# Context attention with its scores computed twice: once plain for the maxima, once with keys on partitions and the maximum taken off inside the product

## The chip, the cores and the metric

One core of a Trainium2 chip runs the whole program in one launch. The metric is the device time of one execution in microseconds (us), lower is better. PE is TensorE, DVE is VectorE, ACT is ScalarE, POOL is GpSimd, SP is the queue that issues most transfers.

## The reference, cut to what matters

The program is a chain of eight residual layers over x of shape (8, 256, 256). The change touches the third alone, an attention in which each of 256 tokens of a batch looks at 256 context tokens and the batch's own 256 tokens. There is no mask in this layer.

```python
def _L1_xattn_ref(x, context, w_qkv, w_proj, b_proj):    # x is layer-normed, (8, 256, 256)
    ...
    q, k, v = (qkv[0], qkv[1], qkv[2])                    # 16 heads of 16
    ...
    k = jnp.concatenate([extra_k, k], axis=2)             # 512 keys
    v = jnp.concatenate([extra_v, v], axis=2)
    attn = jnp.einsum('bhnd,bhmd->bhnm', q * scale, k)
    attn = jax.nn.softmax(attn, axis=-1)
    out = jnp.einsum('bhnm,bhmd->bhnd', attn, v)
    return out @ w_proj.T + b_proj
```

## The kernel before, in words

Activations lie with features on partitions. `context_attention_layer` first runs a layer norm, then one block in which all engines stream through the eight batches. The block is written by `attention_stream`; names of its tiles begin with `ca_`.

The work is cut into iterations: 8 per batch (R), 64 in all (NR). An iteration takes 128 queries (half of a batch's) and four heads, which lie on the four 32-row strips of the partitions: strip u holds heads 2u and 2u+1 of its half, 16 rows each, and the iteration takes the even or the odd one of each strip. The four score products of 128 queries by 512 keys go to four PSUM banks, one per head.

- **PE** makes the four scores (`scores`, line 753), each on its own strip of 32 rows. In batch 0 the operands are plain (`ca_k`, `ca_qz`, where the other head's 16 rows of queries are zero). From batch 1 on they are `HalfStack`'s: queries and keys are split into a rounded part and a rest, both parts of a head stand in one strip, and two products per head in the faster float32r type make one score. Then PE turns the exponentials, 16 transposes of 128x128 per iteration (`turn`, line 767), and every second iteration multiplies them with the values (`values`, line 791), 16 products, each on its own 32 columns of the array.
- **DVE** takes the negated maximum of each score row (line 963) and copies two of the four turned banks of an iteration to SBUF (line 969). **ACT** makes the exponential with the maximum as its bias and the row sum as a second output (line 896) and copies the other two turned banks (line 905).
- The reciprocal of the sums is widened on POOL (line 722), turned by PE (line 810), copied by ACT and multiplied into the output by DVE (line 997). `project` (line 1298) and the addition to the stream (line 1311) follow.
- `HalfStack` costs POOL two casts and three subtractions a batch (lines 1382 to 1394) and SP 24 small transfers a batch that move 16-row halves within SBUF (lines 1403 and 1411).
- The next batch's queries, keys and values (`front`, PE lines 1324 and 1340) are made in iterations 0, 4 and 6 of a batch.

Each engine's order is written out by hand. An engine executes in order, and a wait stops all that stands behind it. A transposing or score product that refills a bank waits for whoever read it last:

```python
for u in range(u0, u0 + GA):
    if n > 0:
        pe.wait_ge(exped, 4 * (n - 1) + u + 1)     # scores: bank u is free when its exponential is done
...
pe.wait_ge(exped, 4 * n + last + 1)                # turn: needs the exponential
pe.wait_ge(copied_v if f % 2 == 0 else copied_a, (fill - 2) // 2 + 1)
```

## Time and profile before

| | |
|---|---|
| median of 3 runs | 2622.49 us (2622.3 to 2631.82) |
| the profiled execution's own time | 2618.37 us |
| its span, first to last instruction | 2616.5 us |
| TensorE's mean granted clock | 0.964 of full |
| the block with the change, first score to last addition | 463.44 to 799.40, 335.96 us |

### The profile page before, as it was taken

What the parts mean: (1) busy time and instruction counts of PE and PEld (TensorE: products, weight loads), DVE (VectorE), ACT (ScalarE), POOL (GpSimd) and SP (SyncE); (2) the same over time, 40 slices, a digit from 0 to 9 for tenths busy, and PEclk for the clock granted to TensorE, in tenths of its full rate; (3) what the DMA queues carried; (4) which work ended last, traced back from release to release, by engine and by line L of the source; (5) the groups of instructions that cost most, each with busy time, mean ns of one, the idle gap of its engine ahead of it and who ended that gap; (6) DMA issues with size and microseconds to landing.
All of it is one profiled execution on the core that took longest, in us unless ns stands there. A gap on an engine that the chain in (4) does not pass through costs nothing. (4 is left out here: it accounts for less than half of the span.)

```text
span 2616.5 us, 38185 instructions
## 1 busy us (share of the span) xinstructions
PE 2261.1 (86%) x14797; PEld 1623.2 (62%) x14797; DVE 1313.9 (50%) x2690; ACT 985.1 (38%) x2815; POOL 175.7 (7%) x227
## 2 busy tenths in 40 slices
PE   6778887899988999989999999997998888773884
PEld 4455565566655666666666666665886666552773
DVE  6456565688885344433554454456443554543003
ACT  3245564677773111121333233344221444323222
POOL 0000000122200000000000000003001000002003
PEclk8979999999999999999999999998999999997997
DMA  3000000122112000021000000001002000004332
GB/s 118 17 1 1 1 1 22 42 53 50 38 29 97 0 1 1 1 83 40 9 9 9 9 9 1 1 1 29 1 1 71 25 17 19 1 1 142 127 131 69
DMA packets 62833, 83.43 MB, mean 32 GB/s; under 512 B 10936, under 2 KB 49088, under 8 KB 61760
## 3 DMA queue, kind: packets, MB, share of 16 engines
q1 hardware_dynamic: 61120, 76.80, 9.5%
q0 software_dynamic: 1536, 4.20, 0.6%
q8 instruction: 121, 1.98, 0.3%
q14 instruction: 56, 0.46, 0.1%
HBM read 65.24 MB, written 8.39 MB: 28 GB/s over the span
## 5 line engine op out<-in xcount | busy, mean ns | idle before, releaser
L896 ACT ACTIVATE ca_prob<-bank,ca_nmax 128x512 f32<-128x512 f32 x256 | 174.0, 690 | 75.0 <-DVE ca_nmax L963 75.0
L896 ACT ACTIVATE na_prob<-bank,na_nmax 128x257 f32<-128x257 f32 x256 | 118.0, 474 | 192.3 <-DVE na_nmax L963 192.3
L963 DVE TENSOR_REDUCE ca_nmax<-bank 128x1 f32<-128x512 f32 x256 | 164.2, 683 | 42.0 <-PE bank L753 42.0
L1596 PE MATMUL bank<-rf_W,rf_h 128*128 128x256 f32 x768 | 170.8, 379 | 0.0
L1585 PE MATMUL bank<-XN,rf_W 128*128 128x512 f32 x384 | 170.1, 593 | 0.0
L1596 PEld LDWEIGHTS bank<-rf_W,rf_h 128*128 128x128 f32 x768 | 146.0, 190 | 33.0 <-issue 14.8
L896 ACT ACTIVATE ra_prob<-bank,ra_nmax 128x256 f32<-128x256 f32 x256 | 118.2, 482 | 105.3 <-DVE ra_nmax L963 105.3
L1640 ACT ACTIVATE rf_r<-bank 128x512 f32<-128x512 f32 x96 | 57.3, 597 | 261.1 <-PE bank L1585 261.1
L767 PE MATMUL bank<-cst,ca_prob 128*128 128x128 f32 x1024 | 141.5, 280 | 7.6 <-DVE ca_pT L969 5.9
L767 PEld LDWEIGHTS bank<-cst,ca_prob 128*128 128x128 f32 x1024 | 111.8, 142 | 54.1 <-issue 45.4
L963 DVE TENSOR_REDUCE na_nmax<-bank 128x1 f32<-128x257 f32 x256 | 90.9, 417 | 91.5 <-PE bank L753 91.5
L1786 PE MATMUL bank<-na_cxT,na_Wkv 128*128 128x256 f32 x512 | 117.8, 383 | 5.6 <-DVE na_q L1780 5.6
L1585 PEld LDWEIGHTS bank<-XN,rf_W 128*128 128x128 f32 x384 | 72.4, 190 | 78.6 <-issue 77.3
L1904 PE MATMUL bank<-sf_h,sf_W 128*128 128x512 f32 x512 | 120.1, 395 | 0.0
L1692 DVE TENSOR_TENSOR rf_h<-rf_r 128x512 f32<-128x512 f32 x96 | 66.1, 692 | 104.4 <-ACT rf_r L1640 104.4
L1798 PE MATMUL bank<-na_Wkv,na_cxT 128*128 128x512 f32 x256 | 115.4, 595 | 0.0
L1786 PEld LDWEIGHTS bank<-na_cxT,na_Wkv 128*128 128x128 f32 x512 | 95.1, 190 | 25.9 <-DVE na_q L1780 11.9
L1904 PEld LDWEIGHTS bank<-sf_h,sf_W 128*128 128x128 f32 x512 | 96.0, 188 | 23.5
L233 PE MATMUL bank<-ln_rstd,cst 128*128 128x128 f32 x352 | 51.9, 291 | 51.7 <-DVE ln_rstd L319 51.7
L969 DVE COPY ca_pT<-bank 128x512 f32<-128x512 f32 x128 | 87.6, 684 | 17.1 <-PE bank L767 16.7
L1705 DVE SCALAR_TENSOR_TENSOR rf_acc<-bank,rf_comb,rf_acc 128x256 f32<-128x256 f32 x112 | 49.0, 479 | 90.9 <-PE bank L1596 90.9
L963 DVE TENSOR_REDUCE ra_nmax<-bank 128x2 f32<-128x512 f32 x128 | 82.1, 683 | 22.1 <-PE bank L753 22.1
(404 smaller groups left out, 4349.3 us busy)
## 6 DMA issues: line engine op xcount, KB each, us to landing
xl_w<-in_L_ffn_w SPq DMA_DIRECT2D x16, 1024.0 KB, 7.5
dp_cx<-in_ctx_tok SPq DMA_DIRECT2D x4, 1024.0 KB, 14.7
ca_v<-in_ctx_values SPq DMA_DIRECT2D x8, 512.0 KB, 4.7
rf_W<-in_L_ffn_w SPq DMA_DIRECT2D x8, 512.0 KB, 9.1
na_Wkv<-in_L_xattn_Wkv SPq DMA_DIRECT2D x1, 4096.0 KB, 16.0
na_cxT<-in_ctx SPq DMA_DIRECT2D x8, 512.0 KB, 3.4
ma_cxT<-in_ctx SPq DMA_DIRECT2D x8, 512.0 KB, 3.3
ca_q_halves<-ca_q_halves SPq DMA_DIRECT2D x112, 32.0 KB, 2.0
```

Source lines behind the costliest of these rows:

```text
L233: mm = pe.matmul(bank[:, c * P:(c + 1) * P], pick[:, c * P:(c + 1) * P], of, start=True, stop=True)
L767: mm = pe.transpose(TB[f % 2][:, j * P:(j + 1) * P], prob[:, n % 2, u, c0:c0 + P], ident)
L896: e = act.activation(prob[:, n % 2, u, hh * keys:(hh + 1) * keys], S[u][:, hh * keys:(hh + 1) * keys], ACT.Exp, bias=nmax[:, n % 2, u, hh: ...
L963: v.tensor_reduce(nmax[:, n % 2, u], S[u][:, 0:W].rearrange("p (h k) -> p h k", h=per), AX.X, ALU.max, negate=True).then_inc(maxed, 1)
L969: v.tensor_copy(o, TB[f % 2][:].rearrange("p (j q) -> p j q", j=4)).then_inc(copied_v, 1)
L1585: mm = pe.matmul(g.bank[n % 3][:], W1[:, k, c * P:(c + 1) * P], g.XN[:, k, gi * GT:(gi + 1) * GT], start=(k == 0), stop=(k == KD - 1))
L1596: mm = pe.matmul(output(i, t), h[:, n % 8, t * P:(t + 1) * P], W2[:, n % CH], start=(n == own[0]), stop=(n == own[-1]), skip_group_check=True)
L1640: act.activation(r[:, n % 3], g.bank[n % 3][:], ACT.Relu).then_inc(relu, 1)
L1692: v.tensor_tensor(h[:, n % 8], r[:, n % 3], r[:, n % 3], ALU.mult).then_inc(squared, 1)
L1786: mm = pe.matmul(bank[:, m * N:(m + 1) * N], Wkv[:, k, (m0 + m) * P:(m0 + m + 1) * P], cxT[:, b % 2, k], start=(k == 0), stop=(k == KC - 1))
L1798: mm = pe.matmul(bank[:], cxT[:, b % 2, k, t * P:(t + 1) * P], Wkv[:, k, INNER + half * 512:INNER + (half + 1) * 512], start=(k == 0), sto ...
L1904: mm = pe.matmul(g.bank[m % 4][:], W1[:, k, m * P:(m + 1) * P], h[:, k, s], start=(k == 0 and s == 0), stop=(k == C1 - 1 and s == 1))
```

## The change: what it does

`attention_stream` loses its `stack` argument, `HalfStack` goes, and the layer calls a new function, `key_major_stream`, with the same 64 iterations plus ten to drain it.

- The scores are made once as in the old batch 0 (plain operands, 128 queries by 512 keys, float32), for the maxima alone. They use a ring of three banks (0 to 2), which they share with one transpose per iteration.
- DVE writes the negated maxima of the four heads into four columns of an otherwise zero tile `ca_Z` (128x128). PE turns it once (`turn_maxima`), and DVE adds it to the queries: `ca_qa` (`shift_queries`). The maximum of a head then stands in a row of the other head's half of the strip. POOL forms a second copy of the keys, `ca_kf`, in which that row is 1.
- Three iterations later PE makes the scores again with keys on partitions: 128 keys by all 256 queries, the maximum already taken off (`turned_score`). Two tiles of keys per head and iteration fill a bank of a ring of three (3 to 5). ACT makes the plain exponential of a bank, 128x512, straight into `ca_pT`. Nothing is turned or copied behind it, and no sum is taken by ACT.
- The values' empty columns hold 0.25, so that the product with the values (8 per iteration) yields the sums as rows of the output bank. Per half batch ACT copies that bank, two transfers take the sums to 64 partitions each, DVE makes the reciprocals, a third transfer takes them to 8 rows, PE spreads them in one product, and DVE multiplies. POOL masks and adds the two halves of the output.

On PE each iteration has two mixed groups: two scores on two strips, and two heads of turned scores, two tiles of keys each, on the other two. In code (waits for a batch's start left out):

```diff
+            def score(n, u):
+                ...
+                if at[e] >= 3:
+                    pe.wait_ge(taken, at[e] - 2)
+                pe.matmul(score_bank(e)[:], qz[32 * u:32 * u + 32, b % 2, odd, m, i * P:(i + 1) * P],
+                          kk[32 * u:32 * u + 32, b % 2, m, :], start=True, stop=True).then_inc(scored, 1)
+            def turned_score(t, j, c):
+                ...
+                if c == 0:
+                    if pos >= 3:
+                        pe.wait_ge(exped, pos - 2)
+                    pe.wait_ge(taken, at[("z", 2 * (t // 2) + 1)] + 1)
+                tile = 2 * (t % 2) + c
+                mm = pe.matmul(g.bank[3 + pos % 3][:, c * N:(c + 1) * N],
+                               kf[32 * u:32 * u + 32, b % 2, m, odd, tile * P:(tile + 1) * P],
+                               qa[32 * u:32 * u + 32, odd], start=True, stop=True, skip_group_check=True)
+            def pair(n, first_unit):
+                t = n - 3
+                ...
+                if n < NR:
+                    score(n, first_unit)
+                    score(n, first_unit + 1)
+                if 0 <= t < NR:
+                    for c in range(2):
+                        turned_score(t, j0, c)
+                        turned_score(t, j0 + 1, c)
+            def turn_maxima(n):
+                e = ("z", n)
+                pe.wait_ge(taken, max(at[e] - 2, at[("s", n, 3)] + 1))
+                pe.transpose(score_bank(e)[:, 0:P], Z[:, (n // 2) % 2, n % 2], ident).then_inc(scored, 1)
+            for n in range(ITER):                       # PE
+                pair(n, 0)
+                if 1 <= n <= NR:
+                    turn_maxima(n - 1)
+                for use in slots[n][0]:                 # spread, project
+                    shared(use)
+                pair(n, 2)
+                if 0 <= n - 4 < NR:
+                    values(n - 4)
+                for use in slots[n][1]:                 # front
+                    shared(use)
+            for n in range(ITER):                       # DVE
+                if n < NR:
+                    maximum(n, 0)
+                    maximum(n, 1)
+                if 1 <= n <= NR:
+                    shift_queries(n - 1)
+                for use in slots[n][0]:
+                    shared(use)
+                if n < NR:
+                    maximum(n, 2)
+                    maximum(n, 3)
+                ...                                     # reciprocal of a half batch
+                for use in slots[n][1]:
+                    shared(use)
-        stack = HalfStack(g, sb, kk)
-        attention_stream(g, ctx, "ca", 16, 16, groups, 2 * N, front, (0, 4, 6), q_of, k_of,
-                         ...
-                         stack=stack)
+        key_major_stream(g, ctx, wl, 3, load, front, (0, 4, 6), qz, kk, vv, project(Wp, KD), add_to_stream(g, bias))
```

`at[e]` is a score's or a turned maximum's place in the order s0, s1, z, s2, s3 of an iteration, and its bank is `at[e] % 3`.

How PE's order changes, in the middle of a batch: before, two iterations of the stream (a score product per head and part, then transposes).

```order
L753 MATMUL bank<-ca_k_halves,ca_q_halves 128x512 x8
L767 MATMUL bank<-cst,ca_prob 128x128 x16
L753 MATMUL bank<-ca_k_halves,ca_q_halves 128x512 x8
L767 MATMUL bank<-cst,ca_prob 128x128 x8
L791 MATMUL bank<-ca_pT,ca_v 32x256 x16
L767 MATMUL bank<-cst,ca_prob 128x128 x8
```

Of the change, one iteration at the same place: L1497 is a plain score, L1509 a turned one, L1537 the turned maxima, L1563 the spread of the reciprocals, L1548 the values.

```order
L1497 MATMUL bank<-ca_k,ca_qz 128x512 x2
L1509 MATMUL bank<-ca_qa,ca_kf 128x256 x4
L1537 MATMUL bank<-cst,ca_Z 128x128
L1563 MATMUL bank<-ca_inv_rows,cst 128x256
L1497 MATMUL bank<-ca_k,ca_qz 128x512 x2
L1509 MATMUL bank<-ca_qa,ca_kf 128x256 x4
L1548 MATMUL bank<-ca_pT,ca_v 32x256 x8
```

The 16 transposes of an iteration are one, the eight float32r products are four plain ones, and eight turned scores have come. They stand behind the second pair of plain scores.

DVE's order before, some two iterations with the multiplication of a batch's output (L997):

```order
L963 TENSOR_REDUCE ca_nmax<-bank 128x1 x2
L969 COPY ca_pT<-bank 128x4x128
L997 TENSOR_TENSOR ca_outT<-bank,ca_spread 128x512
L963 TENSOR_REDUCE ca_nmax<-bank 128x1 x2
L969 COPY ca_pT<-bank 128x4x128
L963 TENSOR_REDUCE ca_nmax<-bank 128x1 x2
L1311 SCALAR_TENSOR_TENSOR X<-bank,ca_bias,X 128x256 x2
```

And of the change, from the addition to the queries (L1642) to the first maxima of the iteration after the one in which the next batch's queries are taken (L1307):

```order
L1642 TENSOR_TENSOR ca_qa<-ca_qz,bank 128x128
L1659 TENSOR_TENSOR ca_outT<-bank,ca_data 128x256
L1632 TENSOR_REDUCE ca_Z<-bank 128x1 x2
L1307 TENSOR_SCALAR ca_qz<-bank,cst 128x512 x2
L1632 TENSOR_REDUCE ca_Z<-bank 128x1 x2
```

The copies of turned banks are gone, a small addition per iteration has come, and the queries of the next batch, two operations in place of one, stand ahead of the maxima.

## Rows read from the trace of the kernel before

**Rows 1.** The cores.

```profile
core 0: 2616.5 us, clock 0.964
```

**Rows 2.** Stretches: from:to, length, each engine's busy us (instructions), clock, DMA.

```profile
463.44:503.90 40.46, 33.76 (x268) 21.19 (x272) 27.68 (x46) 26.85 (x72) 7.95 (x6) 0.96 0.15 27
503.90:543.90 40.00, 36.95 (x364) 26.78 (x356) 32.55 (x56) 31.13 (x81) 8.56 (x7) 1.00 0.21 47
763.90:799.40 35.50, 27.11 (x280) 18.25 (x280) 22.30 (x37) 21.21 (x54) 0.61 (x1) 1.00 0.00 1
463.44:799.40 335.96, 299.62 (x2856) 211.72 (x2856) 261.40 (x437) 250.94 (x655) 60.45 (x50) 0.99 0.17 37
```

**Rows 3.** Groups of instructions between 460 and 800 us.

```profile
L896 ACT ACTIVATE ca_prob<-bank,ca_nmax 128x512 f32<-128x512 f32 x256 | 174.0, 690 | 75.0 <-DVE ca_nmax L963 75.0
L963 DVE TENSOR_REDUCE ca_nmax<-bank 128x1 f32<-128x512 f32 x256 | 164.2, 683 | 42.0 <-PE bank L753 42.0
L767 PE MATMUL bank<-cst,ca_prob 128*128 128x128 f32 x1024 | 141.5, 280 | 7.6 <-DVE ca_pT L969 5.9
...
L969 DVE COPY ca_pT<-bank 128x512 f32<-128x512 f32 x128 | 87.6, 684 | 17.1 <-PE bank L767 16.7
L905 ACT ACTIVATE ca_pT<-bank 128x512 f32<-128x512 f32 x128 | 77.0, 601 | 2.8 <-PE bank L767 2.8
...
L753 PE MATMUL bank<-ca_k_halves,ca_q_halves 32*128 32x512 f32 x448 | 41.4, 439 | 21.0 <-ACT ca_prob L896 21.0
...
L1298 PE MATMUL bank<-ca_outT,ca_Wp 128*128 128x256 f32 x64 | 15.7, 389 | 1.6 <-DVE ca_outT L997 1.6
L1340 PE MATMUL bank<-ca_Wqkv,XN 128*128 128x256 f32 x64 | 15.1, 379 | 0.0
```

**Rows 4.** Timeline of an iteration in batch 2: start, length, engine, work.

```profile
582.13 0.74 PE L753 MATMUL bank<-ca_k_halves,ca_q_halves 32*128 32x512 f32 x8 [0.52 <-ACT ca_prob L896]
...
583.82 1.93 PE L791 MATMUL bank<-ca_pT,ca_v 128*32 128x256 f32 x32
...
587.01 0.74 PE L753 MATMUL bank<-ca_k_halves,ca_q_halves 32*128 32x512 f32 x8 [0.23 <-ACT ca_prob L896]
```

**Rows 5.** Timeline of an iteration in batch 0, plain scores.

```profile
473.52 1.14 PE L753 MATMUL bank<-ca_k,ca_qz 32*128 32x512 f32 x8 [0.71 <-ACT ca_prob L896]
...
474.60 1.09 PE L767 MATMUL bank<-cst,ca_prob 128*128 128x128 f32 x8
474.65 1.29 DVE L963 TENSOR_REDUCE ca_nmax<-bank 128x1 f32<-128x512 f32 x2 [1.59 <-PE bank L753]
...
475.86 0.68 DVE L969 COPY ca_pT<-bank 128x512 f32<-128x512 f32 x1
...
476.69 1.40 PE L767 MATMUL bank<-cst,ca_prob 128*128 128x128 f32 x8 [1.00 <-DVE ca_pT L969]
```

**Rows 6.** Stretches of batch 0 around a change of clock, columns as in Rows 2.

```profile
475.79:479.20 3.41, 1.66 (x12) 1.18 (x16) 2.54 (x5) 3.35 (x10) 0.00 (x0) 1.00 0.25 54
479.20:482.60 3.40, 3.40 (x20) 1.77 (x16) 2.14 (x4) 1.42 (x5) 0.00 (x0) 0.50 0.18 38
```

**Rows 7.** Timeline, the taking of batch 0's queries and the block's last work.

```profile
459.25 1.41 DVE L1460 TENSOR_SCALAR ca_qz<-bank,cst 128x512 f32<-128x512 f32 x2 [4.15 <-PE bank L1324]
...
791.92 1.93 PE L791 MATMUL bank<-ca_pT,ca_v 128*32 128x256 f32 x32 [0.78 <-ACT ca_pT L905]
...
798.52 0.88 DVE L1311 SCALAR_TENSOR_TENSOR X<-bank,ca_bias,X 128x256 f32<-128x256 f32 x2 [2.15 <-PE bank L1298]
```

**Rows 8.** A small DVE addition's nearest neighbour, another layer's.

```profile
L1008 DVE TENSOR_TENSOR ra_rq<-ra_rq,cst 128x80 f32<-128x80 f32 x16 | 3.2, 239 | 0.3
```

**Rows 9.** DMA issues: tiles, queue, count, KB each, median us to landing.

```profile
ca_k_halves<-ca_k_rest SPq DMA_DIRECT2D x56, 64.0 KB, 2.3
```

More of the change, by code:

```diff
@@ L53, in shape_constants @@
     parts["even16"] = np.concatenate([0.25 * ((p // 16) % 2 == 0), 0.25 * ((p // 16) % 2 == 1)], axis=1)
+    parts["keep_one"] = np.concatenate([p % 32 != 16, p % 32 == 16, p % 32 != 0, p % 32 == 0], axis=1)
+    parts["head_row"] = (f // 16 == 2 * (p % 4) + p // 4)
     parts["half5"] = np.where(p < REG, 0.5, 1.0)
@@ L558, in attention_stream @@
                      wl, n_weights, mask=None, own_keys=False, load=None, n_loads=0, load_after=None, null=None, reg=None,
-                     stack=None,
                      divide=False):
@@ L684, in _ @@
                     if b >= 2:
-                        if stack is not None:
-                            stack.move_queries(sp, b)
                         load_after(sp, b - 2, ready, ready_at, valued, R)
@@ L689, in _ @@
                         d.then_inc(ld[b % 2], 16)
-                    if stack is not None and b >= 1:
-                        if b == 1:
-                            stack.move_queries(sp, b)
-                        stack.move_keys(sp, b)
             sp.wait_ge(wl, 16 * n_weights)
@@ L697, in _ @@
         def _(po):
-            def split_keys_and_queries(b):
-                wait_freed(po, ("front", b, 0))
-                if b >= 2:
-                    po.wait_ge(scored, 4 * R * (b - 1))
-                stack.split_queries(po, b)
-                po.wait_ge(ld[b % 2], 16 * n_loads * (b // 2 + 1))
-                stack.split_keys(po, b, slice(0, N))
-                wait_freed(po, ("front", b, 1))
-                stack.split_keys(po, b, slice(N, 2 * N))
             for n in range(NR):
                 f, r2 = divmod(n, RF)
-                if stack is not None and n % R == 0 and n // R + 1 < B:
-                    split_keys_and_queries(n // R + 1)
                 if null is not None:
@@ L735, in scores @@
                         pe.wait_ge(ld[b % 2], 16 * n_loads * (b // 2 + 1))
-                    if stack is not None and b >= 1:
-                        stack.wait_stacked(pe, b)
                 for u0 in range(0, 4, GA):
@@ L745, in scores @@
                             pe.matmul(S[u][:, 0:W], ml, mr, start=True, stop=False, skip_group_check=True)
-                    parts = 2 if stack is not None and b >= 1 else 1
                     for hh in range(per):
-                        for part in range(parts):
-                            for u in range(u0, u0 + GA):
-                                i, a, hs = unit(n, u)
-                                q = q_of(hs[hh], i, b) if parts == 1 else q_of(hs[hh], i, b, part)
-                                last = hh == per - 1 and part == parts - 1
-                                mm = pe.matmul(S[u][:, hh * keys:(hh + 1) * keys], q, k_of(hs[hh], i, b),
-                                               start=(mask is None and part == 0), stop=last, skip_group_check=True)
-                                if last:
-                                    mm.then_inc(scored, 1)
+                        for u in range(u0, u0 + GA):
+                            i, a, hs = unit(n, u)
+                            mm = pe.matmul(S[u][:, hh * keys:(hh + 1) * keys], q_of(hs[hh], i, b), k_of(hs[hh], i, b),
+                                           start=(mask is None), stop=(hh == per - 1), skip_group_check=True)
+                            if hh == per - 1:
+                                mm.then_inc(scored, 1)
             def turn(n, f):
@@ L1425, in context_attention_layer @@
         bias = sb("bias", [P, KD])
-        qz = sb("qz", [P, 2, KD, N])
+        qz = sb("qz", [P, 2, 2, KD, N])
         kk = sb("k", [P, 2, KD, 2 * N])
@@ L1438, in prepare @@
             for j in range(2):
-                po.memset(vv[:, j, 2:4], 0.0).then_inc(zeroed, 1)
+                po.memset(vv[:, j, 2:4], 0.25).then_inc(zeroed, 1)
             po.wait_ge(zeroed, 2)
@@ L1447, in load @@
                                A["ctx_values"][b * N:(b + 1) * N, :].rearrange("(t p) d -> p t d", p=P))
[L1449 to L1489 removed]
+        front = qkv_front(g, Wqkv, qz, g.c("even16"), lambda b: kk[:, b % 2, :, N:2 * N], lambda b: vv[:, b % 2, 2:4])
+        key_major_stream(g, ctx, wl, 3, load, front, (0, 4, 6), qz, kk, vv, project(Wp, KD), add_to_stream(g, bias))
 def routed_ffn_layer(g):
@@ L2542 @@
     lay["L2_null_values"] = nv.reshape(P, 128)
-    cv = _np.zeros((T, 8, 4, 16), _np.float32)
+    cv = _np.full((T, 8, 4, 16), 0.25, _np.float32)
     cv[:, :, 0] = c[:, D:].reshape(T, 8, 2, 16)[:, :, 0]
```

331 lines of the change are left out of this document (258 added, 73 removed).

## Prediction

> **What bounds the kernel now.** I read the cores first: one core, 2616.5 us, clock 0.964 [rows 1]; the execution's own time is 2618.4 us, 4.1 below the median of the three runs. Then the stretches of the block [rows 2]. It lasts 335.96 us, and a batch in the middle takes 40.0 us, in which PE is busy 36.95, DVE 32.55, ACT 31.13 and POOL 8.56. PE is the bound, though not by much. The groups of instructions [rows 3] say what PE does: transposes of the exponentials 141.5 us of 299.6, scores 41.4, the front, the values and the projection. The timeline [rows 4] shows an iteration from score to score: 587.01 - 582.13 = 4.88 us. PE's waits there are short (0.52, 0.23), because while one iteration's maxima and exponentials are made, PE turns those of the iteration before: 2.2 us of work of its own that does not depend on them. That cover is what the reader is to keep in mind.
>
> **What goes.** Per iteration 16 transposes (141.5/64 = 2.2 us of PE), two copies by DVE (87.6/64 = 1.37) and two by ACT (77.0/64 = 1.20) [rows 3], eight float32r products (0.74 us, [rows 4]), POOL's splits and SP's 24 transfers a batch. POOL and SP were off the path.
>
> **What comes on PE.** A plain score group stands in batch 0 [rows 5]: four heads on four strips, two passes each, start at 473.52, and the next work of PE starts at 474.60: 1.08 us. A mixed group of the change fills the same four strips with as many columns (512 on two of them, 2 x 256 on the other two), so it should take 1.08 as well, if the two kinds overlap as four alike do. In the mixed group two more waits stand between the strips' products, and no row prices them; between nothing and 0.2 us I take 0.12, so 1.20. Two groups are 2.3 to 2.4 us. The turned maxima are one transpose, 1.09/8 = 0.14 [rows 5]. The values are half of 1.93 per iteration [rows 4], 0.97, the same per head as before. PE's own work is then 2.2 + 0.14 + 0.97 = 3.3 us against 0.74 + 2.2 + 0.97 = 3.9 before. By work alone the change saves 0.6 us an iteration.
>
> **What comes as a wait.** The second group's second score, s3, refills the bank of s1, three places earlier in the ring, and so waits until DVE has taken the maximum of s1. The turned scores of the second group stand behind s3 in PE's queue, the values behind those, the front behind the values. So PE's chain of an iteration, without front, is:
> - first group's start to DVE's first maximum: 474.65 - 473.52 = 1.13 [rows 5];
> - two maxima: 1.29 [rows 5];
> - DVE's end to PE's start: 475.86 + 0.68 = 476.54, to 476.69 = 0.15 [rows 5];
> - s3 and the turned scores behind it: 1.20 (1.08 at the least);
> - the values: 0.97; then the next first group finds its banks free (the maximum of s2 ended about 0.9 us before).
>
> Together S = 4.74 us (4.62 to 4.9). PE stands still for some 1.3 us in the middle, with only s2 under way in part of it. The transposes that covered this wait before are what the change removes; the turned scores could cover it, but stand behind it.
>
> **Off the path.** DVE's addition to the queries is 128x128; its nearest row is 128x80 in 0.24 us [rows 8], and DVE is idle there. ACT's exponential loses its sum and bias, between 0.60 (a copy of the same bank) and 0.69 [rows 3]; four are 2.4 to 2.8 us of 4.74. The ring of exponential banks waits for exponentials made 1 us or more before, in the worst case by 0.1. The transfers of the sums: 2.3 us to landing for 64 KB moved within SBUF [rows 9]; two hops, a copy and a reciprocal are about 7 us and have five iterations. If that cover went, DVE's next maxima would wait behind the reciprocal; I see no shortage. The spread, 0.5 us, fits in PE's gap.
>
> **The sum over the block.**
> - 60 iterations (4 to 63) at 4.74: 284.4.
> - Front: 21 products of 15.1/8 = 1.89 [rows 3] stand behind the values, on the path; one lies under DVE's work at the start: 37.8.
> - Taking the queries: two DVE operations in 1.41 [rows 7] where the next maximum is due after 1.13, so 0.4 late, six times: 2.4.
> - Projection 15.7/8 = 1.96 [rows 3] in a gap of about 1.35: 0.6, six times: 3.6.
> - Iterations 0 to 2, DVE's four maxima and an addition: 3 x 3.2 = 9.6; iteration 3, S without values: 3.8.
> - Iterations 64 to 66, turned scores, exponentials, values: 3 x 3.8 = 11.4.
> - The end: last exponentials and values, copy, two hops at some 2.4, reciprocal, spread, multiplication, projection, addition: 11.5. Before, the last values to the end took 799.40 - 791.92 = 7.5 [rows 7].
>
> Sum 364.5 against 335.96: +28.5. On the execution's own 2618.4 that is 2647; beside the median, 2651.
>
> **Rivals.**
> *PE stays the bound* (0.10, faster). If the wait for DVE is covered, a batch costs PE 8 x 3.3 + 5.7 (front) + 2.0 + 1.0 = 35.1 us of work in place of 36.95; with the old idle time of 3 us, 38.1 against 40.0. Over 7.5 batches that is -14, and POOL and SP give nothing: 2608. For it speaks that DVE and ACT each lose over 1 us an iteration, against it the ring of three banks. It decides at S: 60 S + 80 = 336 gives S = 4.26, so the gap would have to be 0.5 us shorter than I make it.
> *About no change* (0.12). The gap closes part of the way, by s2 and the spread lying in it and groups nearer 1.0; S of 4.2 to 4.4 gives 2619 to 2631, 2622 where it breaks even.
> *The clock falls* (0.15, slower still). In batch 0 PE was busy 1.66 of 3.41 us, and in the next 3.40 us the granted clock was 0.50, the lower of the two levels, 1.2 GHz [rows 6]; the middle batches, with PE busy 92%, kept 1.00 [rows 2]. The change brings an idle gap in each iteration. Each such 3.40 us gives up 1.7; once a batch is +14, 2665, once in three iterations +34, 2685.
> *The passes don't overlap in mixed groups* (0.08, far slower). If every product waited for both passes of the one ahead of it in program order, s0 and s1 would need 1.5 us and the turned scores another 0.75, 2.25 a group. The second group would still start at 1.13 + 1.29 + 0.15 = 2.57, and the chain is then 2.57 + 2.25 + 0.97 = 5.8, +1.05 x 60: 2714. Four heads alike show the opposite: eight passes of about 0.5 us each in 1.08 [rows 5].
> The Trainium skill, "TensorE: Matmul & The Clock Gate", step-by-step list of Part 2, says that only weight loads are pulled ahead and that the "MATMULs themselves stay in program order". By that rule the group in batch 0 would take about 2.5 us; the trace disagrees with 1.08, and the sum stays with the trace.
>
> **How the numbers follow.** My forecast has 0.55, and its own range is 2638 to 2668: S from 4.62 to 4.9 is -7 to +10, the ends and the front a few us. The rivals have 0.10, 0.12, 0.15 and 0.08. The range of 8 in 10 leaves out the faster case and the passes that don't overlap, which is 0.18, and reaches through the clock's case and most of no change: 2624 to 2690. What a measurement of this kernel can tell from no change is 0.5%, 13 us: faster below 2609, slower above 2636. Faster: 0.10. Same: 0.12 and the lower edge of my own, 0.17. Slower: 0.73.
>
> **What the profile of the changed kernel would show.** PE idle before L1497, ended by DVE's maxima (L1632), once an iteration and about 0.6 to 1.3 us long: over 50 us in all. From a first group to the next without front, 4.7 us. A mixed group of 1.1 to 1.2 us from its first start to PE's next work. DVE and ACT each below 30 us of a batch's 44. No waits for the transfers of sums except at the end. Clock near 1.00 in the middle batches. It is wrong if the idle time before L1497 is small, if a group takes over 1.5 us, or if the clock falls in the middle batches.

## The result, and the profile after

The changed kernel takes 2675.6 us (median of 4 runs, 2673.61 to 2677.25). The kernel before, timed with it, takes 2627.15 us (2622.3 to 2633.11, 4 runs). The ratio is 1.0183, 95% interval 1.0154 to 1.0212, so the change costs 48.5 us where 28.5 were forecast. That lies in the wide range of 2624 to 2690 us, but above my own forecast's, which ended at 2668. The direction was right. The steady part of the block was right too, and its start and end were not.

The first view is the cores of the changed kernel, beside [rows 1].

```profile
core 0: 2674.7 us, clock 0.955
```

The second is its windows, columns as in [rows 2]: the first 42 us of the block, two batches in the middle, and the block.

```profile
466.54:508.90 42.36, 39.68 (x197) 22.85 (x198) 20.81 (x36) 9.28 (x17) 2.49 (x4) 0.72 0.00 1
508.90:553.56 44.66, 40.90 (x360) 24.57 (x362) 25.03 (x48) 19.16 (x35) 8.09 (x10) 1.00 0.07 19
598.22:642.88 44.66, 42.01 (x368) 25.59 (x368) 26.12 (x51) 19.16 (x35) 8.10 (x10) 1.00 0.07 20
466.54:845.42 378.88, 349.25 (x2888) 210.05 (x2888) 207.62 (x396) 152.67 (x279) 61.23 (x76) 0.96 0.05 14
```

The block takes 378.88 us against 335.96, +42.9. A middle batch takes 44.66 against 40.0 at a full clock, with DVE and ACT busy 26 and 19 us of it, so no engine but PE could be the bound by its work alone. The first 42 us ran at a mean clock of 0.72.

The third view is the groups of instructions of the block.

```profile
L1497 PE MATMUL bank<-ca_k,ca_qz 32*128 32x512 f32 x512 | 183.5, 663 | 22.9 <-DVE ca_Z L1632 21.8 <-DVE ca_v L1326 1.1
L1632 DVE TENSOR_REDUCE ca_Z<-bank 128x1 f32<-128x512 f32 x256 | 165.1, 686 | 110.5 <-PE bank L1497 109.4
L1509 PE MATMUL bank<-ca_qa,ca_kf 32*128 32x256 f32 x1024 | 154.1, 405 | 0.7 <-ACT ca_pT L1592 0.7
L1592 ACT ACTIVATE ca_pT<-bank 128x512 f32<-128x512 f32 x256 | 138.9, 594 | 199.1 <-PE bank L1509 199.1
L1548 PE MATMUL bank<-ca_pT,ca_v 128*32 128x256 f32 x1024 | 69.2, 389 | 0.0
...
L1497 PEld LDWEIGHTS bank<-ca_k,ca_qz 32*128 32x128 f32 x512 | 56.9, 188 | 80.7 <-DVE ca_Z L1632 63.7 <-issue 15.5 <-DVE ca_v L1326 1.4
```

DVE waits for scores (109.4 us), and the weight loads of the scores wait for DVE (63.7 us): each waits for the other. PE itself shows only 21.8 us of idle time before L1497, because a score on another strip is still under way in part of the wait. The timeline of one iteration in batch 2 shows that.

```profile
602.75 0.70 PE L1497 MATMUL bank<-ca_k,ca_qz 32*128 32x512 f32 x2
...
602.77 0.70 PE L1509 MATMUL bank<-ca_qa,ca_kf 32*128 32x256 f32 x4
...
603.29 0.59 PE L1497 MATMUL bank<-ca_k,ca_qz 32*128 32x512 f32 x2
603.30 0.60 PE L1509 MATMUL bank<-ca_qa,ca_kf 32*128 32x256 f32 x4
...
603.83 0.33 PE L1537 MATMUL bank<-cst,ca_Z 128*128 128x128 f32 x1
603.91 1.29 DVE L1632 TENSOR_REDUCE ca_Z<-bank 128x1 f32<-128x512 f32 x2 [1.57 <-PE bank L1497]
...
604.65 0.29 PEld L1497 LDWEIGHTS bank<-ca_k,ca_qz 32*128 32x128 f32 x2 [0.28 <-DVE ca_Z L1632]
...
605.25 0.18 PEld L1497 LDWEIGHTS bank<-ca_k,ca_qz 32*128 32x128 f32 x1 [0.31 <-DVE ca_Z L1632]
...
605.36 0.79 PE L1509 MATMUL bank<-ca_qa,ca_kf 32*128 32x256 f32 x4
...
605.81 1.29 DVE L1632 TENSOR_REDUCE ca_Z<-bank 128x1 f32<-128x512 f32 x2
...
606.51 1.07 PE L1548 MATMUL bank<-ca_pT,ca_v 128*32 128x256 f32 x16
607.51 1.99 PE L1300 MATMUL bank<-XN,ca_Wqkv 128*128 128x256 f32 x8
609.44 0.70 PE L1497 MATMUL bank<-ca_k,ca_qz 32*128 32x512 f32 x2
```

Read from the top: the group starts, 1.16 us later DVE begins, 1.29 later both maxima are taken, s3's weights load at 605.25, the turned scores behind it and s3 end at 606.51, and the values take 1.00 to the front at 607.51. That is 4.76 us where 4.74 were forecast.

The fourth view is the windows around the changes of clock at the start and the end of the block.

```profile
462.82:469.66 6.84, 4.98 (x22) 2.76 (x21) 2.66 (x6) 0.60 (x1) 4.08 (x6) 1.00 0.02 7
469.66:473.07 3.41, 3.41 (x8) 2.32 (x8) 0.68 (x1) 0.00 (x0) 0.00 (x0) 0.50 0.00 0
473.07:476.48 3.41, 2.63 (x11) 1.22 (x11) 2.80 (x6) 0.00 (x0) 0.00 (x0) 1.00 0.00 0
476.48:496.96 20.48, 20.40 (x82) 11.77 (x79) 9.88 (x17) 4.34 (x8) 0.00 (x0) 0.50 0.00 1
...
831.48:838.31 6.83, 2.74 (x36) 1.16 (x34) 0.68 (x2) 1.56 (x3) 2.54 (x3) 1.00 0.03 5
838.31:845.13 6.82, 4.94 (x10) 3.02 (x10) 1.02 (x3) 0.00 (x0) 0.00 (x0) 0.50 0.00 0
```

The granted clock was 0.50, the 1.2 GHz level, for 23.9 us in the first iterations and for 6.8 us over the last spread and projection. Each time PE had been idle for part of the stretch ahead. Before, batch 0 had one such stretch of 3.40 us [rows 6].

**Where the 42.9 us are.** I marked each iteration by its turned maxima (L1537). From the sixth of them to the last, 58 iterations, the chip took 317.3 us and my sum has 316.8. The steady part was right. From the first score to the sixth turned maxima it took 37.1 us and my sum has 26.0: +11.1. From the last turned maxima to the last addition the sum was 2.8 short. With 0.5 in the middle that is the whole 14.4 between the forecast +28.5 and +42.9. Outside the block the start comes 3.1 us later than before. The layer norm behind it takes as long as before. The 16 products of the next layer's router (L1566, now L1796) take 1.5 us more, 3.32 us at a mean clock of 0.54 where they took 1.85 us at 1.00.

The two profiled executions differ by more, 58.9 us. Of that, 9.3 lie in the last expert layer, which took 225.1 us in the profile before and 234.4 in this one. The change doesn't touch it, and in profiles of other kernels below it took 227 to 238, so the profile before was a short one of its kind: 2618.37 us beside a median of 2627.15. The layer's length goes with its granted clock: 225.1 us at a mean of 0.86, 227.4 at 0.85 (e7), 234.4 at 0.82, 237.9 at 0.80 (e4). No edit was made there, so this is seen and not tested. I compare medians for the total and records for the block.

### The profile page after: what moved, and what is told of

Its sections match the earlier page's. It is cut to its first block and busy times, and to the rows that moved or that the text cites. A ratio compares the mean times of both kernels' runs of the same rounds, so it can differ in the third digit from the quotient of the medians.

```text
span 2674.7 us, 37814 instructions
## 1 busy us (share of the span) xinstructions
PE 2323.0 (87%) x14829; PEld 1630.3 (61%) x14829; DVE 1260.7 (47%) x2650; ACT 887.8 (33%) x2439; POOL 180.1 (7%) x257
## 5 line engine op out<-in xcount | busy, mean ns | idle before, releaser
L1632 DVE TENSOR_REDUCE ca_Z<-bank 128x1 f32<-128x512 f32 x256 | 165.1, 686 | 110.5 <-PE bank L1497 109.4
L1592 ACT ACTIVATE ca_pT<-bank 128x512 f32<-128x512 f32 x256 | 138.9, 594 | 199.1 <-PE bank L1509 199.1
L1497 PE MATMUL bank<-ca_k,ca_qz 32*128 32x512 f32 x512 | 183.5, 663 | 22.9 <-DVE ca_Z L1632 21.8
L1509 PE MATMUL bank<-ca_qa,ca_kf 32*128 32x256 f32 x1024 | 154.1, 405 | 0.7 <-ACT ca_pT L1592 0.7
L1497 PEld LDWEIGHTS bank<-ca_k,ca_qz 32*128 32x128 f32 x512 | 56.9, 188 | 80.7 <-DVE ca_Z L1632 63.7
L1509 PEld LDWEIGHTS bank<-ca_qa,ca_kf 32*128 32x128 f32 x1024 | 99.7, 188 | 6.2 <-ACT ca_pT L1592 2.3
```

What stands on the lines that cost most here:

```text
L1497: pe.matmul(score_bank(e)[:], qz[32 * u:32 * u + 32, b % 2, odd, m, i * P:(i + 1) * P], kk[32 * u:32 * u + 32, b % 2, m, :], start=True, s ...
L1509: mm = pe.matmul(g.bank[3 + pos % 3][:, c * N:(c + 1) * N], kf[32 * u:32 * u + 32, b % 2, m, odd, tile * P:(tile + 1) * P], qa[32 * u:32 * ...
L1592: act.activation(pT[:, t % 2, TURN[j]].rearrange("p c q -> p (c q)"), g.bank[3 + pos % 3][:], ACT.Exp)\
L1632: v.tensor_reduce(Z[:, odd, n % 2, col:col + 1], score_bank(e)[:], AX.X, ALU.max, negate=True)\
```

## The experiments

All start from the changed kernel. I give them by what they tell apart, not in the order in which they ran. In the table, "against before" is the difference to the median of the kernel before, timed with it on the same chip, "58 iterations" is from the sixth to the last turned maxima, "start" from the first score to the sixth, "block" from the first score to the last addition, in us.

| kernel | median | against before | ratio, 95% | start | 58 iterations | block |
|---|---|---|---|---|---|---|
| changed | 2675.60 | +48.5 | 1.0154 to 1.0212 | 37.1 | 317.3 | 378.9 |
| e1 | 2663.97 | +36.1 | 1.0086 to 1.0148 | 34.9 | 294.6 | 360.8 |
| e2 | 2670.45 | +42.6 | 1.0142 to 1.0177 | 37.0 | 306.6 | 368.0 |
| e3 | 2643.36 | +15.5 | 1.0032 to 1.0075 | 30.9 | 290.0 | 345.4 |
| e4 | 2671.98 | +44.1 | 1.0133 to 1.0179 | 28.6 | 317.3 | 369.9 |
| e5 | 2704.55 | +81.1 | 1.0277 to 1.0324 | 35.6 | 347.3 | 407.2 |
| e6 | 2676.30 | +52.8 | 1.0174 to 1.0217 | 37.2 | 317.7 | 379.5 |
| e7 | 2667.58 | +44.1 | 1.0152 to 1.0200 | 30.6 | 318.0 | 373.1 |
| e8 | 2666.85 | +43.4 | 1.0138 to 1.0183 | 28.6 | 317.3 | 368.3 |
| e9 | 2646.21 | +19.9 | 1.0042 to 1.0095 | 34.6 | 284.9 | 344.8 |
| e10 | 2659.16 | +32.8 | 1.0089 to 1.0138 | 35.4 | 301.3 | 362.9 |
| e11 | 2644.67 | +18.3 | 1.0046 to 1.0084 | 28.1 | 301.3 | 353.5 |
| e12 | 2679.28 | +53.0 | 1.0158 to 1.0215 | 35.6 | 320.3 | 380.4 |
| e13 | 2657.63 | +31.9 | 1.0064 to 1.0129 | 30.8 | 302.0 | 359.6 |
| e14 | 2647.05 | +21.3 | 1.0045 to 1.0092 | 27.6 | 290.6 | 344.4 |
| e15 | 2635.72 | +10.0 | 1.0014 to 1.0044 | 26.9 | 290.6 | 341.3 |
| e16 | 2663.52 | +37.8 | 1.0090 to 1.0156 | 27.7 | 312.1 | 367.6 |

Theory A is the prediction's: PE stands still in each iteration because a score must wait for the maximum of the score three places earlier in its ring of banks. The main rival is that PE's own work bounds the iteration. A second question is the clock at the ends.

**e3, half as much work for DVE.** A maximum looks at 256 of the 512 keys, so its result can be another one.

```diff
-                v.tensor_reduce(Z[:, odd, n % 2, col:col + 1], score_bank(e)[:], AX.X, ALU.max, negate=True)\
+                v.tensor_reduce(Z[:, odd, n % 2, col:col + 1], score_bank(e)[:, 0:N], AX.X, ALU.max, negate=True)\
```

> Each maximum is taken over the first 256 of the 512 scores of its row (this leaves out part of the maximum; the scores themselves are all made). A maximum should take about 0.41 us for 0.68, and two back to back about 0.76 for 1.29. Theory A: the two maxima lie on the chain once per iteration, so -0.5 us x 60 = -30, about 2645. Theory B (PE is the bound) or C (the clock): 2670 to 2680, as DVE is idle half the time.

The timeline of e3, two maxima and the turned maxima of two iterations:

```profile
599.69 0.33 PE L1537 MATMUL bank<-cst,ca_Z 128*128 128x128 f32 x1
599.77 0.76 DVE L1632 TENSOR_REDUCE ca_Z<-bank 128x1 f32<-128x256 f32 x2 [1.16 <-PE bank L1497]
...
603.91 0.33 PE L1537 MATMUL bank<-cst,ca_Z 128*128 128x128 f32 x1
```

Two maxima take 0.76 us in place of 1.29, and the iteration 4.22 in place of 4.76: 0.54 shorter, as much as the maxima, although DVE was busy for little more than half of the time. The maxima are on PE's path, and the whole came to -33 us: 27 of the 33.5 us by which the block shrank are in the 58 iterations, 6 at its start, where 13.7 us ran at a clock of 0.50 for 23.9 in the changed kernel.

**e12, work for PE where it stands still.**

```diff
+                if 3 < n < NR:
+                    free = 4 * (n - 3) + 2
+                    pe.wait_ge(exped, free - 2)
+                    pe.matmul(g.bank[3 + free % 3][:, 0:N], ident, g.XN[:, 0, 0:N], start=True, stop=True, skip_group_check=True)
                 pair(n, 2)
```

> The changed kernel with one unread 128x256 product (0.5 us of PE) in each of iterations 4 to 63, between the turned maxima and the second group. If PE stands idle there for DVE (theory A), the 60 products cost nothing: 2676, within 2 us of the changed kernel. If PE's work bounds the iteration (rival B), they cost up to 60 x 0.5 = 30 us: 2706.

An iteration stayed at 4.76 us. The 60 products cost 3.0 us over the 58 iterations, nearly all of it in the seven iterations with a projection, where PE's gap is filled already (6.01 us there, the changed kernel has 5.58). The rival's 30 us are not there. The total came out 4.5 us above the changed kernel's, more than the 2 expected.

**e1, the values moved into the gap.**

```diff
                 for use in slots[n][0]:
                     shared(use)
-                pair(n, 2)
                 if 0 <= n - 4 < NR:
                     values(n - 4)
+                pair(n, 2)
```

> The values product of an iteration is issued between the turned maxima and the second group instead of behind it; nothing else moves. Theory A (the chain: first group, two maxima, second group, values, each waiting for the one before): the values, 0.97 us, now lie in PE's idle gap of about 1.3 us, the iteration falls from 4.76 to about 3.9 us, over 60 iterations -52 us, so about 2623, no slower than the kernel before. Theory B (PE itself is the bound in the steady part, groups of mixed strips simply cost more than the transposes did): the order changes nothing, 2670 to 2680. Theory C (the whole excess is the clock at the start and end of the block): the same 2670 to 2680.

This missed: -12 us where theory A said -52. The timeline of e1 shows where the gap's place was taken.

```profile
603.74 0.70 PE L1497 MATMUL bank<-ca_k,ca_qz 32*128 32x512 f32 x2
...
604.90 2.60 DVE L1632 TENSOR_REDUCE ca_Z<-bank 128x1 f32<-128x512 f32 x4 [1.63 <-PE bank L1497]
...
605.64 0.18 PEld L1497 LDWEIGHTS bank<-ca_k,ca_qz 32*128 32x128 f32 x1 [0.74 <-DVE ca_Z L1632]
...
606.90 0.33 PE L1537 MATMUL bank<-cst,ca_Z 128*128 128x128 f32 x1
607.16 1.07 PE L1548 MATMUL bank<-ca_pT,ca_v 128*32 128x256 f32 x16
608.16 0.70 PE L1497 MATMUL bank<-ca_k,ca_qz 32*128 32x512 f32 x2
```

The group of 603.74 is now the second one. Behind it comes the next iteration's first group with nothing between, and its second score needs the bank of s2. So the wait stands at s1, for the first maximum of the pair. The iteration is 1.16 + 0.65 + 0.18 to s1, a group of 1.17, the turned maxima 0.26 and the values 1.00: 4.42 us. The projection lost its gap too: the iteration with it went from 5.58 to 6.58. My expectation had moved the work and forgotten the wait on the other side of the ring.

**e2, the second group turned round.**

```diff
-                if n < NR:
+                if n < NR and first_unit == 0:
                     score(n, first_unit)
                     score(n, first_unit + 1)
                 if 0 <= t < NR:
                     ...
+                if n < NR and first_unit == 2:
+                    score(n, first_unit)
+                    score(n, first_unit + 1)
```

> In the second group of an iteration the turned scores are issued ahead of the two plain scores; nothing else moves. The turned scores then fill the gap, but the two plain scores still wait for both maxima and the values still wait for them. Theory A: the chain keeps 1.13 + 1.29 + 0.15 + 1.08 + 0.97 = 4.6 of its 4.76 us, so -7 to -10 us, 2666 to 2669. A rival (what stands behind the waiting score is what costs, so PE gains all the work that is moved ahead of it, about 1 us an iteration): about 2615. Theory B or C: 2670 to 2680.

An iteration took 4.55 us in place of 4.76, and the 58 iterations 10.7 less. The median went down by 6, a little less than the 7 to 10 expected. The turned scores cover part of the wait, as expected.

**e5 and e6, the fourth score late.** e5 issues s3 behind the values and the front:

```diff
                 pair(n, 2)                                  # now without score(n, 3)
                 if 0 <= n - 4 < NR:
                     values(n - 4)
                 for use in slots[n][1]:
                     shared(use)
+                if n < NR:
+                    score(n, 3)
```

> From the changed kernel: the fourth score of an iteration, s3, is issued behind the values (and the front), directly ahead of the next iteration's first group, all else as in the changed kernel. Theory A (the ring of three score banks stops PE at s3, and e1 missed because with the values in the gap the same wait stood at the next s1, behind s2's maximum): s3 is now reached after about 1.15 + 0.26 + 0.7 + 1.0 = 3.1 us, when its bank has been free since 2.57, so PE's wait before s3 goes. What is left is the turned maxima, which need the maximum of s3: s3's group about 1.3, its maximum 1.13 + 0.65 + 0.15 behind s3's start, so 0.6 of idle time; iteration 1.95 + 0.26 + 0.7 + 1.0 = 3.9 us without front, about 6 us a batch less than 44.66 with front and projection on the path, 2625 to 2640 in all. Rival B (the iteration is bound by the work of PE and DVE together, and e3 was faster only because DVE had less work): the iteration stays above 4.3, and the time above 2650.

e6 also issues four of the eight products with the values between `pair(n, 0)` and `turn_maxima(n - 1)`.

> As e5, and the values of an iteration in two halves of four products: one between the first group and the turned maxima, one behind the second group. Theory A: the first half (0.5 us) covers most of the 0.6 us that PE would wait for the turned maxima in e5; iteration 3.4 to 3.7 us without front, a batch 36.5 to 38.5, total 2605 to 2625, so under the kernel before. Rival B: as for e5, no faster than 2650. Rival C: another ring stops it next (the exponentials' banks, or s1 behind the maximum of s2), iteration 3.8 to 4.0 as in e5, total 2625 to 2640.

Both missed, e5 by 65 us and e6 by 51. The timeline of e5, in an iteration behind one with a front:

```profile
608.96 0.69 DVE L1635 TENSOR_REDUCE ca_Z<-bank 128x1 f32<-128x512 f32 x1 [3.49 <-PE bank L1497]
...
610.23 1.28 DVE L1635 TENSOR_REDUCE ca_Z<-bank 128x1 f32<-128x512 f32 x2
610.96 0.18 PEld L1497 LDWEIGHTS bank<-ca_k,ca_qz 32*128 32x128 f32 x1 [1.11 <-DVE ca_Z L1635]
```

The one maximum at 608.96 is that of the late s3. It stands ahead of the next iteration's maxima in DVE's queue, so s2, which refills the bank of s0, waits for DVE to reach it: from the group's start 1.16, two maxima 1.29, 0.15, a group 1.2 and the values 1.0 are 4.8 us, the same chain as before with another score at its end (4.76 measured). With a front in the iteration the maxima come later again. Those longer waits had a second effect: the clock fell in the middle of the block. It was 0.50 for 30.7 us of e5's 58 iterations, for example for 13.7 us from 523.10 on, where PE had been idle for 1.6 of the 6.8 us before. So a part of e5's loss is the clock and not the chain. In e6 half of the values lies in the wait, 4.38, and it loses that in the iterations with front and projection.

**e9 and e10, the values split around the second group.**

```diff
                     turn_maxima(n - 1)
+                if 0 <= n - 4 < NR:
+                    values(n - 4, range(0, 4))              # e10: range(0, 6)
                 for use in slots[n][0]:
                     shared(use)
                 pair(n, 2)                                  # now s2, turned scores, s3
                 if 0 <= n - 4 < NR:
-                    values(n - 4)
+                    values(n - 4, range(4, 8))              # e10: range(6, 8)
```

> From the changed kernel: four of an iteration's eight products with the values are issued ahead of the second group, between the turned maxima and it; and in the second group the turned scores stand between s2 and s3. Theory A (PE's chain runs over two waits of one ring, s3 behind the maximum of s1 and the next s1 behind that of s2; e1, e5 and e6 each moved PE's work so that the other wait took over): the start of the first group to s3 is 1.13 + 1.29 + 0.15 = 2.57 as before, and behind it stand s3 alone, about 1.0, and half of the values, 0.5: 4.05 us without front against 4.76, about 40 us in the block, 2633 to 2640. Rival B (a mixed group can't be cut up without loss, or s3 alone takes as long as a group): 4.4 and more, 2655 or above.

> As e9 with six of the eight products ahead of the second group. Theory A: 2.57 + 1.0 + 0.25 = 3.85 us an iteration, 5 to 12 us below e9, 2625 to 2632; if the next s1 then waits for the maximum of s2, as in e1, 4.0 to 4.1 and the same time as e9.

e9's iterations came as worked out: 3.99 and 4.12 us, a batch 40.2, 34 us less in the block. The total is 29 us under the changed kernel's and 6 above the range expected. e10 was slower, and not 5 to 12 us faster. Its timeline:

```profile
604.77 0.63 PE L1551 MATMUL bank<-ca_pT,ca_v 128*32 128x256 f32 x4
604.85 1.29 DVE L1638 TENSOR_REDUCE ca_Z<-bank 128x1 f32<-128x512 f32 x2 [0.17 <-PE bank L1497]
...
605.33 0.96 PE L1497 MATMUL bank<-ca_k,ca_qz 32*128 32x512 f32 x2
605.67 0.18 PEld L1509 LDWEIGHTS bank<-ca_qa,ca_kf 32*128 32x128 f32 x1
...
606.85 0.33 PE L1540 MATMUL bank<-cst,ca_Z 128*128 128x128 f32 x1
607.11 1.06 PE L1551 MATMUL bank<-ca_pT,ca_v 128*32 128x256 f32 x12
608.10 0.69 PE L1497 MATMUL bank<-ca_k,ca_qz 32*128 32x512 f32 x1
```

Six products ahead delay s2 and its maximum, and only two products behind them don't cover it. The first group then takes 1.52 us (605.33 to 606.85) for s1 waits in it, and 1.52 + 0.26 + 0.99 + 1.08 + 0.56 are the 4.41 measured. The balance matters to a tenth of a microsecond.

**e13 to e16, four banks for the scores.** The six banks are shared out as four and two, with PE's order as it was:

```diff
-        return g.bank[at[e] % 3]
+        return g.bank[at[e] % 4]
...
-                if at[e] >= 3:
-                    pe.wait_ge(taken, at[e] - 2)
+                if at[e] >= 4:
+                    pe.wait_ge(taken, at[e] - 3)
...
-                    if pos >= 3:
-                        pe.wait_ge(exped, pos - 2)
+                    if pos >= 2:
+                        pe.wait_ge(exped, pos - 1)
...                                         # banks and waits of the others likewise
```

> The changed kernel with its six banks shared out otherwise: four for the ring of plain scores and turned maxima, two for the turned scores (three and three before). PE's order is unchanged. Theory A (the ring of three sets the iteration): s3 now waits for the maximum of s0 instead of that of s1, one maximum of 0.65 us earlier, so the chain loses up to 0.65: from 4.76 to 4.1 to 4.3 us an iteration (the last turned scores then wait for the exponential of the second, about 2.5 us behind the start), 20 to 35 us in the block: 2640 to 2655. Rival B (the ring of two for the turned scores stops PE instead): 4.6 and more, 2665 or slower.

> The rings of e13 with PE's order of e9 (half of the values ahead of the second group, turned scores between s2 and s3). Theory A: PE's own work of an iteration is about 3.5 us, and the wait left is covered in part: 3.6 to 3.8 us, 2610 to 2630. Rival B: no better than e9, 2646, because PE then waits for exponentials.

> e15 with six of the eight products with the values ahead of the second group instead of four. In the ring of three that was slower (4.41 us an iteration against 4.05), since the next s1 then waits for the maximum of s2. With four banks that wait is one maximum shorter: 3.5 to 3.7 us an iteration, the time of e15 or up to 5 us below it. If the ring still stops s1, above e15.

The timeline of e13:

```profile
592.81 0.70 PE L1497 MATMUL bank<-ca_k,ca_qz 32*128 32x512 f32 x2
...
593.97 1.29 DVE L1632 TENSOR_REDUCE ca_Z<-bank 128x1 f32<-128x512 f32 x2 [1.79 <-PE bank L1497]
594.08 1.08 ACT L1592 ACTIVATE ca_pT<-bank 128x512 f32<-128x512 f32 x2 [0.54 <-PE bank L1509]
...
594.71 0.18 PEld L1497 LDWEIGHTS bank<-ca_k,ca_qz 32*128 32x128 f32 x1 [0.27 <-DVE ca_Z L1632]
...
595.33 1.02 PE L1509 MATMUL bank<-ca_qa,ca_kf 32*128 32x256 f32 x5
...
596.28 1.07 PE L1548 MATMUL bank<-ca_pT,ca_v 128*32 128x256 f32 x16
```

s3 loads 1.90 us behind the group's start (594.71 - 592.81) where the changed kernel had 2.50: one maximum less, as theory A says, with nothing changed in what PE, DVE or ACT do. Only 0.29 of it arrives (4.47), since the last turned scores now wait for the second exponential in their ring of two. It ends at 595.16, and they start at 595.33. So e13 fell between the two numbers expected, 4.3 and 4.6. In e14 rival B's number came: 4.25 to 4.28 us, above e9's, and e9's total. In the timeline of e14 turned scores wait for an exponential (L1598) in the first group as well. In e16, which is e15 below with six of the eight products ahead, the iteration is 4.67 where 3.5 to 3.7 was expected, and the total is 28 us above e15's; which wait makes it so long was not looked into. I was wrong that two banks are enough for the turned scores: both rings bind, and a bank given to one is taken from the other.

**e4, e7, e8, e11 and e15, the clock at the ends.** Unread products are put where PE stands still at the ends of the block. e4 is the changed kernel with two in each of the first three iterations:

```diff
+                if n < 3:
+                    for _ in range(2):
+                        pe.matmul(g.bank[3][:, 0:N], ident, g.XN[:, 0, 0:N], start=True, stop=True, skip_group_check=True)
                 pair(n, 2)
```

e7 is e6 with the same. e8 is e4 with ten more ahead of the last spread, e11 is e10 and e15 is e14 with those in the first iterations and eight ahead of the last spread:

```diff
+                if use == ("spread", 2 * B - 1):
+                    for _ in range(10):
+                        pe.matmul(g.bank[3][:, 0:N], ident, g.XN[:, 0, 0:N], start=True, stop=True, skip_group_check=True)
```

> Two products of 128x256 that nobody reads are added in PE's gap in iterations 0, 1 and 2, about 0.95 us each time, where PE waits for the maxima anyway. In the changed kernel the clock was 0.50 for 20.5 us from 476 us on, and iterations 0 to 5 took 11 us more than my sum had for them. If PE's idle time in the iterations without turned scores is what lets the clock fall: the half clock there shortens or goes and the time falls by 5 to 11 us, 2665 to 2670. If the clock falls for another reason, or by chance: no change, 2674 to 2678. On the steady iterations, 4.76 us, it has no effect in any theory.

> e6 with the two unread products of e4 in iterations 0 to 2. Theory A (clock at half in the first iterations costs time): 3 to 8 us below e6. Rival: the same as e6 within 2 us, because e6's start is not the changed kernel's.

> e4 (two unread 128x256 products in iterations 0 to 2 of the changed kernel) and ten more such unread products ahead of the last spread, in PE's idle time of 4.7 us at the end of the block. If PE's idle time is why the clock was 0.50 over the last spread and projection, these take 0.7 and 2.0 us and the layer norm behind them 1.5 less: 3 to 4 us below e4, 2667 to 2669. If the clock there does not follow from PE's idle time: as e4, 2672. The ten products take some 5 us and could hold the spread up by 0.5.

> e10 with the unread products of e8 in iterations 0 to 2 and (eight of them) ahead of the last spread. Theory A, with the clock's part at both ends: 5 to 9 us below e10, which is under the kernel before by 0 to 10 us.

> e14 with the unread products in iterations 0 to 2 and ahead of the last spread. The same edit took 14.5 us from e10's time, though the clock's half intervals there explain about 11 of it: 8 to 14 us below e14. If e14 comes out as theory A says, this one beats the kernel before.

The windows of e4 over the first iterations, and then of e8 over the last spread and projection:

```profile
476.50:497.00 20.50, 18.73 (x143) 11.19 (x142) 12.71 (x24) 8.20 (x15) 1.51 (x2) 1.00 0.00 1
```

```profile
826.50:833.60 7.10, 5.55 (x24) 4.00 (x22) 1.55 (x4) 0.00 (x0) 0.62 (x1) 1.00 0.01 1
```

The clock stays at full in both places. It does so in iterations 3 to 5 too, to which nothing was added. The start of the block shrinks from 37.1 to 28.6 us though PE has six products more to do, the end by 2.0 in e8. None of the six kernels with unread products at the start shows half clock there, and each of the eleven others does, for 10 to 24 us. The end is less clear: e8, e11 and e15 keep the full clock there, while e16, with the same eight products as e15, has 6.8 us at 0.50 over its last iterations.

In the totals, e7 is 8.7 us below e6, e11 14.5 below e10, e15 11.3 below e14, more than expected in e7 and e11 and as expected in e15. e4 and e8 are only 4 and 5 below the changed kernel, so e4 fell short of the 5 to 11 expected, and e8 is one below e4 where 3 to 4 were expected. e11 stayed 18 us above the kernel before, which it was to beat.

The totals don't measure the block's part alone. The blocks shrank by 9.0 us (e4), 10.6 (e8), 6.4 (e7), 9.4 (e11) and 3.1 (e15). The rest of each difference lies in layers that these edits don't touch. Behind the block, e4's profile is 4.5 us longer than the changed kernel's, e15's is 9 us shorter than e14's. That goes with the clock there too: the mean clock of the whole profiled execution is 0.952 in e14 and 0.961 in e15. Within one kernel it is the same: e14's seven runs go from 2653.75 us at 0.951 to 2638.85 at 0.958. Runs of one kernel lie 2 to 15 us apart. Whether the unread products have a part in the clock behind the block is not shown: in three pairs that stretch got shorter, in e4 and e8 it didn't.

The best of all is e15, 2635.72 us, still 1.0029 (1.0014 to 1.0044) of the kernel before. Its block takes 341.3 against 335.96. No version here beats the old kernel.

## Why the prediction was right or wrong

- **The steady iteration: right.** 4.76 us for 4.74, by its own terms 1.16 for 1.13, 1.29 for 1.29, then 605.25 - 603.91 - 1.29 = 0.05 to the load and 0.11 to the turned scores for 0.15, 1.15 for 1.20, 1.00 for 0.97. The front is +1.92 for 1.89; projection and queries together +0.82 for 1.0. (The queries' 0.4 was a slip: 1.41 - 1.13 is 0.28, and the next maximum came 0.27 late.) One sign that I had named didn't come: PE's idle time before L1497 is 22.9 us and not over 50, since a score on another strip is under way in part of each wait. The wait shows in the weight loads, 63.7 us. e3 and e12 show that it is a wait and not PE's work, e13 that the ring's length sets it.
- **The mixed group: right.** 602.75 to 603.83 is 1.08 us for two plain scores and two heads of turned ones on four strips, as for four scores alike [rows 5]. The rival in which every product waits for both passes of the one ahead fell. The sentence of the Trainium skill that I set beside it ("TensorE: Matmul & The Clock Gate", Part 2, step by step), that the "MATMULs themselves stay in program order", speaks of order and not of overlap. I had read it pass by pass, and so read it doesn't hold here for products on different strips: four passes of turned scores start from 602.77 on, ahead of the plain scores' second passes at 603.29, which belong to products that were issued before them. The first passes do start in the order of the program, at 602.75 and 602.77.
- **The step that failed: the terms of the block's start and end, priced at a full clock and, for the first front, at nothing.** "Iterations 0 to 2, DVE's four maxima and an addition: 3 x 3.2 = 9.6; iteration 3, S without values: 3.8" and "The end: ... 11.5" were sized from rows at a full clock. These are the iterations with least to do for PE, and the clock was at 0.50 there for 23.9 and 6.8 us. Start: 37.1 us for 26.0. At a full clock (e4) it is 28.6, so 8.5 of the 11.1 go with the clock. The other 2.6 have two causes. The front of iteration 0, which "lies under DVE's work" in my sum, lies on PE's own path (470.03 to 471.95 in e4): from the first score to the first turned maxima e4 takes 6.1 us where the sum has 4.4. And I took DVE's work for the length of iterations 1 and 2, but they are 4.08 and 4.10 us in e4 for 3.2, because DVE waits for the scores each time. Iteration 3 came as forecast, 3.77 for 3.8, and iterations 4 and 5 were 0.9 shorter than the sum. The wait in iteration 2 of e4:

```profile
479.37 2.60 DVE L1635 TENSOR_REDUCE ca_Z<-bank 128x1 f32<-128x512 f32 x4 [1.29 <-PE bank L1497]
```

  (1.29 + 2.60 for 3.2; the unread products may have a part in it.) End: +2.8, of which e8 gives 2.0 back.
- **The rival of the clock: the mechanism was right, the place wrong.** I looked for it in the middle batches, where each iteration has an idle gap, and put "once a batch" at +14. There the clock kept 1.00 in all iterations of the changed kernel. (In e5, whose waits are longer, it did fall there.) In the changed kernel it fell where the pipeline fills and drains, and took 8.5 + 2.0 us of the block there. The row for it was in the prediction: the one stretch at 0.50 of batch 0 [rows 6] lay in the old kernel's own filling. The Trainium skill ("TensorE: Matmul & The Clock Gate", Part 1, what's actually happening) says that "the default state is throttled, and activity releases the throttle". e4 and e8 agree: work that nobody reads kept the clock at full.
- **The transfers of the sums: right.** No wait for them but at the end, where the spread waits 4.73 us for the last.
- **The base.** The sum was set beside a profile 8.8 us shorter than the median that was measured later. That makes the two profiles stand 58.9 us apart where the medians stand 48.5 apart.

What stays open: how much of the total the clock at both ends is worth in the changed kernel itself. The block's records say 8.5 + 2.0, the medians 4 to 5, and those hold the changing clock of the other layers as well. Why the clock of untouched layers differs from run to run is open too. The stretch at half clock ahead of the block, over the first front (L1300), was left as it is in all kernels.

## What to carry to other kernels

In a ring of banks between two engines, write down for each refill whose reading it waits for, and whose reading stands ahead of that one. Moving work into a gap moves the wait to the next refill unless the work on both sides is balanced: half of the values in the gap gained 29 us, all of them 12, six of eight 16, and a late score lost 33. Price the filling and the draining of a pipeline by iterations of their own and at the clock that so little work gets. A few unread products where TensorE stands still took 3 to 11 us out of the block here. And before a difference of some microseconds in the total is put down to an edit, compare the stage that was edited, and the granted clock of the rest.

## What the runs showed of the hardware

- Six unread 128x256 products of about 0.5 us kept the clock at full over some 20 us that were at half without them (e4). The work added 3 us to PE and the stretch became 8.5 us shorter.
- In the changed kernel's middle batches PE was idle for 2.7 to 3.8 of 44.66 us, a part of it in every iteration, and the clock never fell. In e5 it fell to 0.50 in the middle, first behind 3.40 us in which PE was idle for 0.9 (506.10 to 509.50). At the start of the block 1.9 of 6.84 us idle stood ahead of one fall (462.82 to 469.66) and 0.8 of 3.41 ahead of the next (473.07 to 476.48).
- A layer that no edit touches took 225 to 238 us in the profiles of these kernels, at mean clocks of 0.86 to 0.80. That spread is as large as several of the effects looked for.
